# Node phases with the own products made in the edge passes, biases without matmuls and seven table buffers; a convolution whose weighted marks come from GpSimd

## The chip, the cores and the metric

The kernel runs on 1 core of one Trainium2 chip. A core has TensorE (PE: matmuls, its results go to PSUM), VectorE (DVE), ScalarE (ACT), GpSimd (POOL) and SyncE (SP, which here only issues DMAs), and 16 DMA engines that move data between HBM, the chip's large memory, and SBUF, the core's own. Engines run side by side, each through its own list of instructions, and wait for one another on semaphores. The metric is the device time of one execution in microseconds (us), as the median over runs.

## The reference

Four graph layers over N = 6250 nodes with D = 128 features and E = 106250 edges sorted by destination; each is followed by a residual and a layer norm.

```
x = layernorm(x + [x, mean over edges of x[src]] @ W0)                              # layer 0: sum
x = layernorm(x + relu([x, max over edges of msg] @ U1 + c1) @ U2 + c2)             # layer 1: max
      msg = relu([x[src], x[dst], w] @ W1 + b1) @ W2 + b2
x = layernorm(x + sum over edges and loops of (x @ conv_w)[src] * norm + conv_b)    # layer 2: convolution
      norm = dinv[src] * gate * dinv[dst],  gate = sigmoid(gelu([x[src], x[dst]] @ mlp_w1 + mlp_b1) @ mlp_w2 + mlp_b2)
x = layernorm(x + beta mix of (x @ Wskip + bskip) and attention(q, k, v) over edges) # layer 3: attention
```

## The kernel before

Everything is float32 except masks and marks. Nodes are 49 tiles of 128 (NT), taken in 13 batches of four (BT = 4; the last batch has one tile). Edges are 832 tiles of 128, taken in 208 batches of four (BATCHES). The program is a row of phases with a barrier after each: `edges_sum`, `nodes` 0, `edges_max`, `nodes` 1, `edges_gate`, `edges_conv`, `nodes` 2, `edges_attention`, `nodes` 3. Tile names in a profile begin with L, L2a (the gate) or N (a node phase).

**Edge passes.** Four of them gather one row per edge: GpSimd issues one indirect DMA for each of the 832 tiles (`gatherer`, L513) into a ring of eight batches (DEEP), and the other engines turn, scan and store what arrived. `pipeline` writes the software pipeline: at step s an engine does batch s - lag of each of its stages, in the order of the list. A scan (`running_sum`, L616) adds rows of one destination, steered by a mask that is 1 where an edge has the destination of the edge before it.

**The convolution pass** gathers nothing. `edges_gate` has put the rows x @ conv_w of all edges aside in `sent`, so `edges_conv` streams them back (L670, 256 KB a batch), scales each row and scans. The scale of an edge is its gate weight (`ew`) times dinv of its source, looked up by two sets of marks: `hot_low` (L712, which of 128 lanes) goes through TensorE against the table of dinv (`look`, L687, 12 matmuls a batch) and gives 49 candidates for each edge; `hot_high` (L716) marks the right one; VectorE multiplies (L723), sums (L727) and multiplies by the weight (L732). ScalarE scales the rows (L743) and copies the turned sums out (L633). SP issues four DMAs a batch: the lanes `low` and the `mask` (L752, both bf16 and repeated to 128 partitions, 128 KB each), `sent` (L670) and the store of `back` (L624). All of them have rings of four batches (SLOTS).

**Node phases** (`nodes_on`). GpSimd first issues 49 indirect DMAs that fetch the aggregate of each node (`got`, L1386). It then issues 49 that scatter each node's destination table into `seed` (L1477), four to a batch, each batch once its `comb` buffer is filled. Batches go through PE, VectorE and ScalarE with lags of up to six batches: turn the aggregate (L1505), multiply (phase 0: W0x on the node's own x and W0a on the aggregate, L1519 and L1520; phase 1: U1x and U1a, L1511 and L1512, then U2, L1525), layer norm (VectorE L1394 to L1405, ScalarE L1411 and L1418), turn the new x (L1533, copied to `xT` at L1625), make the tables of the next layer (L1545). Biases are added by further matmuls of three bf16 parts against ones (L1526, L1546, L1693). `keep_tables` (L1634, ScalarE) copies the tables from PSUM to `comb`, a ring of three batches (NSLOTS); it waits until the scatter of three batches before has landed. In phase 2 the node's own row x @ conv_w is read back from HBM (`load_xt`, L1488).

## Time and profile before

| | us |
|---|---|
| median of 3 runs | 5461.31 (5458.39 to 5461.77) |
| the profiled execution | 5471.71 |
| its span, first to last instruction | 5470.0 |
| stage: edges_sum, from 0 to 1059.91 | 1059.9 |
| node phase 0, to 1212.52 | 152.6 |
| edges_max, to 2280.03 | 1067.5 |
| node phase 1, to 2469.09 | 189.1 |
| edges_gate, to 3539.55 | 1070.5 |
| edges_conv, to 4096.05 | 556.5 |
| node phase 2, to 4258.26 | 162.2 |
| edges_attention and node phase 3, to the end | 1211.7 |

A stage here begins with GpSimd's first instruction in it. Over the span PE is busy 66%, VectorE 65%, ScalarE 28%, GpSimd 64%. Such averages hide the stages: each has its own limit, and is read on its own. In the rows below a time stands first, then a duration, the engine (a q behind it means its queue, which issues DMAs), the line, the operation, output<-inputs and the shape; what stands in brackets is the idle time before it and what ended it. `issue` means that the engine waited for nothing that the profile shows.

### The profile page before, as it was taken

The page shows a single profiled execution, that of the slowest core. Times are in us where ns is not written, and L with a number is a line of the kernel's source. Part 1 is how long each engine was busy: PE and PEld are TensorE (multiplying, and loading weights), DVE is VectorE, ACT ScalarE, POOL GpSimd, SP SyncE. Part 2 cuts the span into 40 slices and gives each one's busy share as a digit, 9 for nine tenths or more (in the row PEclk, how much of TensorE's full clock was granted, in tenths as well). Part 3 has the DMA queues.
Part 4 walks back from the last instruction along what each step waited for, and adds up shares of the span by engine and source line. Part 5 has one row for each costly group of instructions (what it writes and reads, how often), then busy time and mean ns, then how long its engine had stood idle before and what let it go on. Part 6 is the DMA issues. An engine that isn't in the chain of part 4 may idle for free. (4 is left out here: it accounts for less than half of the span.)

```text
span 5470.0 us, 86641 instructions
## 1 busy us (share of the span) xinstructions
PE 3630.2 (66%) x19277; PEld 2699.7 (49%) x19277; DVE 3535.5 (65%) x7296; ACT 1505.4 (28%) x3630; POOL 3508.5 (64%) x3697
## 2 busy tenths in 40 slices
PE   4444333466666666677888888766656688888883
PEld 3333333344443444345666666555542466666662
DVE  6555222227888878615777777799883466666667
ACT  1111111132222222232222222266664122222222
POOL 7777777667777777647777777500006777777763
PEclk7555555568888888765555555598885677777775
DMA  7555555436666667426666666599983676677761
GB/s 234 182 183 180 188 186 179 140 92 198 206 209 208 207 208 207 138 63 164 172 170 170 171 170 169 140 307 306 290 277 116 190 215 213 214 212 218 215 187 50
DMA packets 832058, 1031.70 MB, mean 189 GB/s; under 512 B 233279, under 2 KB 544079, under 8 KB 831954
## 3 DMA queue, kind: packets, MB, share of 16 engines
q1 hardware_dynamic: 482964, 483.11, 29.0%
q0 software_dynamic: 144320, 323.10, 22.6%
q10 hardware_dynamic: 204670, 224.39, 11.6%
q8 instruction: 30, 0.49, 0.0%
q14 instruction: 74, 0.61, 0.0%
HBM read 668.65 MB, written 361.50 MB: 188 GB/s over the span
## 5 line engine op out<-in xcount | busy, mean ns | idle before, releaser
L513 POOL DMA_INDIRECT L_gath<-tab,src x832 | 796.4, 957 | 256.5 <-issue 250.9
L513 POOL DMA_INDIRECT L_gath<-in_x,src x832 | 789.1, 948 | 255.9 <-issue 251.8
L513 POOL DMA_INDIRECT L_gath<-tab_kv,src x832 | 788.9, 948 | 253.6 <-issue 240.2
L513 POOL DMA_INDIRECT L2a_gath<-tab_h,src x832 | 788.3, 947 | 253.8 <-issue 253.8
L616 DVE TENSOR_TENSOR_SCAN L_acc<-L_mask,L_acc,L_pT 128x512 f32<-128x512 bf16 x414 | 527.5, 1274 | 568.5 <-PE L_pT L574 567.5
L1386 POOL DMA_INDIRECT N_got<-run,last x196 | 190.0, 969 | 664.2 <-POOLq L116 605.6
L633 ACT ACTIVATE L_back<-L_pB 128x512 f32<-128x512 f32 x624 | 364.3, 584 | 894.5 <-PE L_pB L604 888.5
L574 PE MATMUL L_pT<-ident,L_gath 128*128 128x128 f32 x832 | 227.4, 427 | 558.9 <-DMA L_gath<-in_x,src 550.0
L604 PE MATMUL L_pB<-ident,L_acc 128*128 128x128 f32 x2496 | 522.8, 349 | 0.8 <-DVE L_acc L616 0.5
L604 PEld LDWEIGHTS L_pB<-ident,L_acc 128*128 128x128 f32 x2496 | 412.1, 185 | 154.0 <-issue 151.9
L574 PEld LDWEIGHTS L_pT<-ident,L_gath 128*128 128x128 f32 x832 | 146.3, 214 | 637.8 <-DMA L_gath<-in_x,src 340.1
L810 PE MATMUL L_pM<-L_hid,w_W 128*128 128x512 f32 x416 | 295.2, 799 | 175.6 <-DVE L_acc L842 175.0
L928 PEld LDWEIGHTS L2a_pZ<-w_M,L2a_hid 64*128 64x128 f32 x1664 | 370.1, 325 | 79.5 <-issue 79.5
L928 PE MATMUL L2a_pZ<-w_M,L2a_hid 64*128 64x1 f32 x1664 | 387.7, 351 | 0.0
L820 DVE SCALAR_TENSOR_TENSOR L_sent<-b_W1w,L_weight,L_gath 128x128 f32<-128x128 f32 x832 | 235.7, 344 | 204.8 <-DMA L_gath<-tab,src 204.3
L1181 PE MATMUL L_pR<-L_pv,L_same 128*128 128x132 f32 x1664 | 335.8, 364 | 40.0 <-DVE L_pv L1253 37.0
L851 ACT ACTIVATE L_hid<-L_pre 128x512 f32<-128x512 f32 x208 | 131.0, 630 | 834.9 <-DVE L_pre L835 834.9
L955 DVE TENSOR_TENSOR_SCAN L2a_dest<-L2a_same,L2a_dest,L2a_pS 64x512 f32<-64x512 bf16 x207 | 262.8, 1270 | 143.6 <-PE L2a_pS L915 143.6
L1181 PEld LDWEIGHTS L_pR<-L_pv,L_same 128*128 128x128 f32 x1664 | 293.3, 262 | 64.7 <-DVE L_pv L1253 39.4
L921 PE MATMUL L2a_pA<-ident,L2a_gath 128*64 128x128 f32 x832 | 215.1, 414 | 162.9 <-DMA L2a_gath<-tab_h,src 162.9
L1226 DVE TENSOR_TENSOR L_prod<-L_pQ,L_gath 128x512 f32<-128x512 f32 x208 | 143.8, 691 | 269.6 <-DMA L_gath<-tab_kv,src 217.9
L743 ACT ACTIVATE L_scaled<-L_sent,L_scale 128x128 f32<-128x128 f32 x832 | 265.8, 390 | 184.9 <-DVE L_scale L732 181.5
(283 smaller groups left out, 7276.5 us busy)
## 6 DMA issues: line engine op xcount, KB each, us to landing
run<-L_back ACTq DMA_DIRECT2D x416, 256.0 KB, 4.0
L_seed<-seed SPq DMA_DIRECT2D x416, 256.0 KB
run<-L_back ACTq DMA_DIRECT2D x208, 264.0 KB
L_mask<-same SPq DMA_DIRECT2D x416, 128.0 KB, 3.9
seed<-L_zeros SPq DMA_DIRECT2D x208, 256.0 KB, 4.0
sent<-L2a_gath ACTq DMA_DIRECT2D x208, 256.0 KB, 2.9
L_sent<-sent SPq DMA_DIRECT2D x208, 256.0 KB, 4.6
run<-L_back SPq DMA_DIRECT2D x208, 256.0 KB, 4.5
```

The costliest lines, as they stand in the source:

```text
L513: gp.indirect_dma_start(out=gath[k][:, t, :], out_offset=None, in_=table, in_offset=bass.IndirectOffsetOnAxis(ap=g["src"][:, tile:tile + 1 ...
L574: m = pe.transpose(pT[k % 2][:, cols(t)], gath[k][:, t, :], g["ident"][:, :])
L604: m = pe.transpose(pB[k % 2][:, cols(t)], acc[k][:, cols(t)], g["ident"][:, :])
L616: v.tensor_tensor_scan(acc[k][:, :], mask[k][:, :], pT[k % 2][:, :], start_of(acc, n, k), ALU.mult, ALU.add).then_inc(s_scan, 1)
L633: act.activation(rows(back[k][:, :, :]), pB[k % 2][:, :], ACT.Copy).then_inc(s_back, 1)
L743: a = act.activation(scaled[k][:, t, :], sent[k][:, t, :], ACT.Copy, scale=scale[k][:, t:t + 1])
L810: pe.matmul(pM[k % 2][:, :], w["W2"][:, :], hid[k][:, :], start=True, stop=True).then_inc(s_msg, 1)
L820: a = v.scalar_tensor_tensor(sent[k % SLOTS][:, cols(t)], g["wide"]["W1w"][:, :], weight[:, bass.ds(n * BT + t, 1)], gath[k][:, t, :], ALU ...
L921: m = pe.transpose(pA[k % 2][H, cols(t)], gath[k][:, t, H], g["ident"][:, :])
L928: m = pe.matmul(pZ[k % 2][:, t:t + 1], hid[k % SLOTS][:, cols(t)], w["M2"][:, :], start=True, stop=True)
L955: v.tensor_tensor_scan(dest[k][:, :], same[k][:, :], pS[k % 2][H, :], start_of(dest, n, k), ALU.mult, ALU.add).then_inc(s_dest, 1)
L1181: m = pe.matmul(pR[half][:, at:at + W3], same[k][:, cols(t)], pv[k % 2][:, t, :], start=True, stop=True)
```

## The change

- **Own products in the passes.** x @ W0x is made in `edges_sum`, between stretches of its second half, and added to x in SBUF; x @ U1x + c1 is made at the head of `edges_max` (13 matmuls and 13 ScalarE activations ahead of the pipeline) and written over `xT`; node phase 1 adds it with one VectorE operation a batch (`add_own`). conv_b is added to x at the head of `edges_gate` (13 VectorE adds). In node phase 1 ScalarE writes the rows x @ conv_w over `xT` (`own_rows`), from where phase 2 reads them, without `load_xt`.
- **Biases.** b1, c1 and m1 are the bias operand of an activation; c2 is added to x on VectorE (once a batch in phase 1); the bias of the k, v and q tables is added by VectorE as it takes them out of PSUM (`keep_biased`, four operations a batch in phase 2 in place of ScalarE's four copies). Only bskip stays a matmul.
- **Tables in flight.** `comb` has seven buffers (COMBS). The memset of its padding moves from GpSimd to VectorE, and SP's stores have no lag.
- **Convolution.** GpSimd makes `hot_high` with the gate weight already in it, one operation for each tile (`weigh_high`, 832 in all, 128x49 float32 with two per-partition scalars); VectorE's L716 and L732 are gone. The mask is stored once more as bytes (`same8`) and loaded for four batches at once (256 KB), in a ring of two.

```diff
+            for first, end, parts in stretches:
+                for n in parts:
+                    room(pe, s_added, n, 1)
+                    for t in tiles_of(n):
+                        m = pe.matmul(pX[0][:, cols(t - n * BT)], g["xT"][:, cols(t)], g["w"]["W0x"][:, :], start=True, stop=True)
+                    m.then_inc(s_own, 1)
+                pipeline(pe, end, DEEP, [(0, turn), (2, ret)], first=first)
...
+                    v.tensor_tensor(mine, pX[0][:, 0:m * P].rearrange("p (t f) -> p t f", t=m), mine, ALU.add).then_inc(s_added, 1)
...
-            pipeline(sp, BATCHES, SLOTS, [(0, mask_load(sp, g["low"], low, s_low, s_hotl)), (0, load),
-                                          (2, mask_load(sp, g["same"], mask, s_mask, s_scan)), (8, store_rows(sp, run, back, s_back, s_out))])
+            def load_mask(n, k, r):
+                if k % SLOTS == 0:
+                    room(sp, s_scan, n + SLOTS - 1, DEEP)
+                    sp.sem_inc(s_mgo, 1)
+                    sp.dma_start(mask[k // SLOTS][:, :], g["same8"][bass.ds(n * BE, SLOTS * BE)].unsqueeze(0).to_broadcast([P, SLOTS * BE])).then_inc(
+                        s_mask[k // SLOTS], 16)
+            pipeline(sp, BATCHES, DEEP, [(0, on_short(mask_load(sp, g["low"], low, s_low, s_hotl))), (0, on_short(load)),
+                                         (1, load_mask), (8, on_short(store_rows(sp, run, back, s_back, s_out)))])
...
+            def weigh_high(n, k, r):
+                room(gp, s_part, n, SLOTS)
+                for t in range(BT):
+                    tile = n * BT + t
+                    a = gp.tensor_scalar(hot_high[k][:, t, :], row[:, :], high[:, tile:tile + 1], ew[:, tile:tile + 1], ALU.is_equal, ALU.mult)
+                a.then_inc(s_hoth, 1)
+            steps(BATCHES, SLOTS, [(0, weigh_high)])
...
-            pipeline(v, BATCHES, SLOTS, [(0, hot), (1, pick), (0, hot_of_high), (1, gather_up), (3, running_sum(v, pT, mask, acc, s_turn, s_mask, s_ret, s_scan)),
-                                         (1, times_weight)])
+            pipeline(v, BATCHES, DEEP, [(0, on_short(hot)), (1, on_short(pick)), (3, scan), (1, on_short(gather_up))])
...
+            for n in range(NB):
+                room(pe, s_kept, n, 2)
+                m = len(tiles_of(n)) * P
+                pe.matmul(pB[n % 2][:, 0:m], w["U1x"][:, :], g["xT"][:, n * BE:n * BE + m], start=True, stop=True).then_inc(s_own, 1)
...
-    comb = slot("comb", [P, BT, cw])
+    comb = [ph.sb(f"comb{k}", [P, BT, cw]) for k in range(COMBS)]
...
-            pe.matmul(pU[:, 0:count(n) * P], w["U1x"][:, :], g["xT"][:, flat(n)], start=True, stop=False)
-            pe.matmul(pU[:, 0:count(n) * P], w["U1a"][:, :], aT[k][:, 0:count(n) * P], start=False, stop=True).then_inc(s_u, 1)
+            pe.matmul(pU[:, 0:count(n) * P], w["U1a"][:, :], aT[k][:, 0:count(n) * P], start=True, stop=True).then_inc(s_u, 1)
...
-                    pe.matmul(pY[:, cols(t)], g["xT"][:, cols(n * BT + t)], w["W0x"][:, :], start=True, stop=False)
-                    m = pe.matmul(pY[:, cols(t)], aT[k][:, cols(t)], w["W0a"][:, :], start=False, stop=True)
+                    m = pe.matmul(pY[:, cols(t)], aT[k][:, cols(t)], w["W0a"][:, :], start=True, stop=True)
...
+                v.tensor_tensor(comb[k][:, j, 0:fw], pT[j][:, 0:fw], wide["kvq"][:, :], ALU.add).then_inc(s_comb, 1)
```

**PE in node phase 0.** One step in the middle of the phase, before and after (N_pA: aggregate turned; N_pX: new x turned; N_pY: the layer's result; N_pT: tables).

```order
L1505 MATMUL N_pA<-ident,N_agg 128x128 x4
L1533 MATMUL N_pX<-ident,x 128x128 x4
L1519 MATMUL N_pY<-w_W0x,xT 128x128
L1520 MATMUL N_pY<-w_W0a,N_aT 128x128
...
L1545 MATMUL N_pT<-w_W,xT 128x256
L1546 MATMUL N_pT<-bias,ones 128x128
...
```

```order
L1555 MATMUL N_pA<-ident,N_agg 128x128 x4
L1579 MATMUL N_pX<-ident,x 128x128 x4
L1568 MATMUL N_pY<-w_W0a,N_aT 128x128 x4
L1589 MATMUL N_pT<-w_W,xT 128x256 x4
L1555 MATMUL N_pA<-ident,N_agg 128x128 x4
```

Before, each pair stood four times in a step; of 16 matmuls behind the turn of x eight are left.

**VectorE in node phase 2.** One step before and after (N_st, N_mv, N_inv, N_off: the norm's statistics).

```order
L1580 TENSOR_TENSOR N_base<-x,b_conv_b 128x512
L1582 TENSOR_TENSOR N_base<-N_base,N_part 128x512
L1586 SCALAR_TENSOR_TENSOR N_y<-N_got,N_weight,N_base 128x128 x4
L1394 BN_STATS N_st<-N_y 128x6 x4
L1397 BN_AGGR N_mv<-N_st 128x2 x4
L1404 RECIPROCAL N_inv<-N_std 128x4
L1405 SCALAR_TENSOR_TENSOR N_off<-N_mv,N_inv 128x4
```

```order
L1636 TENSOR_TENSOR N_base<-x,N_part 128x512
L1640 SCALAR_TENSOR_TENSOR N_y<-N_got,N_weight,N_base 128x128 x4
L1448 BN_STATS N_st<-N_y 128x6 x4
L1451 BN_AGGR N_mv<-N_st 128x2 x4
L1458 RECIPROCAL N_inv<-N_std 128x4
L1459 SCALAR_TENSOR_TENSOR N_off<-N_mv,N_inv 128x4
L1656 TENSOR_TENSOR N_comb<-N_pT,b_kvq 128x384 x4
```

The add of conv_b has left the step, and the four table copies that stood on ScalarE (L1634) now end it on VectorE.

**VectorE in the convolution.** One batch of the loop before and after.

```order
L712 TENSOR_SCALAR L_hotl<-L_low,L_lane 128x512
L723 TENSOR_TENSOR L_part<-L_pL,L_hoth 128x196
L716 TENSOR_TENSOR L_hoth<-L_row,L_high 128x196
L727 TENSOR_REDUCE L_found<-L_part 128x4
L616 SCALAR_TENSOR_TENSOR L_acc<-L_mask,L_acc,L_pT 128x512
L732 TENSOR_TENSOR L_scale<-L_found,ew_sb 128x4
```

```order
L754 TENSOR_SCALAR L_hotl<-L_low,L_lane 128x512
L760 TENSOR_TENSOR L_part<-L_pL,L_hoth 128x196
L772 SCALAR_TENSOR_TENSOR L_acc<-L_mask,L_acc,L_pT 128x512
L765 TENSOR_REDUCE L_scale<-L_part 128x4
L754 TENSOR_SCALAR L_hotl<-L_low,L_lane 128x512
```

Six operations a batch have become four; the scale of a batch is still ready only behind the scan (in these listings the scan is printed as SCALAR_TENSOR_TENSOR).

## Rows read from the trace of the kernel before

**Rows 1.** Stages: length, busy us of PE, PEld, DVE, ACT, POOL, clock, DMA share, GB/s

```profile
1059.91:1212.52 152.61, 99.38 (x441) 69.42 (x441) 36.33 (x150) 50.35 (x114) 95.25 (x98) 0.72 0.23 64
...
1212.52:2280.03 1067.51, 676.52 (x2912) 440.53 (x2912) 848.26 (x1456) 232.43 (x416) 796.39 (x833) 0.83 0.68 205
...
2280.03:2469.09 189.06, 134.44 (x444) 73.55 (x444) 44.53 (x164) 56.35 (x126) 97.05 (x102) 0.70 0.20 60
...
3539.55:4096.05 556.50, 365.54 (x4160) 300.31 (x4160) 492.39 (x1254) 366.46 (x1040) 0.26 (x2) 0.87 0.92 294
...
4096.05:4258.26 162.21, 95.47 (x196) 34.91 (x196) 51.16 (x201) 65.94 (x173) 96.59 (x99) 0.58 0.41 119
```

**Rows 2.** The page's groups: busy, mean ns of one | idle before, releasers

```profile
L513 POOL DMA_INDIRECT L_gath<-in_x,src x832 | 789.1, 948 | 255.9 <-issue 251.8 <-DMA src<-in_src 2.6 <-PE L_pT L574 1.5
...
L1477 POOL DMA_INDIRECT seed<-N_comb,first x147 | 145.4, 989 | 163.1 <-ACT N_comb L1634 126.2 <-issue 36.9
```

**Rows 3.** Order of time, PE in node phase 0: start, duration

```profile
1122.12 0.65 PE L1533 MATMUL N_pX<-ident,x 128*128 128x128 f32 x4 [2.30 <-ACT x L1418]
...
1125.53 1.06 PE L1545 MATMUL N_pT<-w_W,xT 128*128 128x256 f32 x2
...
1127.32 0.23 PE L1546 MATMUL N_pT<-bias,ones 3*128 3x128 bf16 x1
...
1127.47 0.70 PE L1545 MATMUL N_pT<-w_W,xT 128*128 128x256 f32 x2
...
1129.04 0.66 PE L1505 MATMUL N_pA<-ident,N_agg 128*128 128x128 f32 x4
...
1132.00 0.66 PE L1533 MATMUL N_pX<-ident,x 128*128 128x128 f32 x4 [2.31 <-ACT x L1418]
```

**Rows 4.** Order of time, PE in node phase 1

```profile
2350.85 0.66 PE L1533 MATMUL N_pX<-ident,x 128*128 128x128 f32 x4 [2.87 <-ACT x L1418]
...
2351.34 1.49 PE L1511 MATMUL N_pU<-xT,w_U1x 128*128 128x512 f32 x2
...
2352.63 1.91 PE L1512 MATMUL N_pU<-N_aT,w_U1a 128*128 128x512 f32 x2
...
2363.51 0.90 PE L1533 MATMUL N_pX<-ident,x 128*128 128x128 f32 x3 [2.88 <-ACT x L1418]
```

**Rows 5.** Order of time, GpSimd and ScalarE in node phase 2

```profile
4159.04 1.02 POOL L1477 DMA_INDIRECT seed<-N_comb,first  x1 [0.30 <-issue]
...
4165.24 1.25 ACT L1634 ACTIVATE N_comb<-N_pT 128x384 f32<-128x384 f32 x3 [14.37 <-DMA seed<-N_comb,first]
```

**Rows 6.** Order of time, VectorE and SP's queue in the convolution

```profile
3803.51 1.27 DVE L616 TENSOR_TENSOR_SCAN L_acc<-L_mask,L_acc,L_pT 128x512 f32<-128x512 bf16 x1
...
3803.93 0.33 SPq L752 DMA_DIRECT2D L_mask<-same  x1
...
3804.51 0.36 SPq L624 DMA_DIRECT2D run<-L_back  x1
...
3805.28 0.35 DVE L716 TENSOR_TENSOR L_hoth<-L_row,L_high 128x196 bf16<-128x196 bf16 x1
...
3805.82 1.27 DVE L616 TENSOR_TENSOR_SCAN L_acc<-L_mask,L_acc,L_pT 128x512 f32<-128x512 bf16 x1
```

**Rows 7.** DMA in the convolution, 400 us: queue share; issues, KB, us to landing

```profile
q1 hardware_dynamic: 88065, 120.29, 94.1%
...
L_mask<-same SPq DMA_DIRECT2D x153, 128.0 KB, 4.4
```

**Rows 8.** Order of time, ScalarE in the convolution: four rows scaled

```profile
3804.94 1.28 ACT L743 ACTIVATE L_scaled<-L_sent,L_scale 128x128 f32<-128x128 f32 x4 [1.30 <-DVE L_scale L732]
```

**Rows 9.** Order of time, GpSimd: an iota, and a fetch beside a VectorE add

```profile
3539.64 0.18 POOL L678 IOTA L_row_i<- 128x49 int32 x1
...
4140.48 0.69 DVE L1580 TENSOR_TENSOR N_base<-x,b_conv_b 128x512 f32<-128x512 f32 x1 [1.08 <-ACT x L1418]
...
4140.76 1.23 POOL L1386 DMA_INDIRECT N_got<-run,last  x1 [0.30 <-issue]
```

More of the change, by code:

```diff
@@ L546, in edges_sum @@
         half = beside.STEPS
+        s_own, s_added = ph.sem("own"), ph.sem("added")
+        turns = [half + j * 2 * DEEP for j in range(5)] + [BATCHES]
+        stretches = [(turns[j], turns[j + 1], range(3 * j, min(3 * j + 3, NB))) for j in range(5)]
         block = ph.block()
@@ L588, in _ @@
             beside.vector_after(v)
-            pipeline(v, BATCHES, DEEP, [(0, scan)], first=half)
+            for first, end, parts in stretches:
+                for n in parts:
+                    need(v, s_own, n)
+                    m = len(tiles_of(n))
+                    mine = g["x"][:, n * BT:n * BT + m, :]
+                    v.tensor_tensor(mine, pX[0][:, 0:m * P].rearrange("p (t f) -> p t f", t=m), mine, ALU.add).then_inc(s_added, 1)
+                pipeline(v, end, DEEP, [(0, scan)], first=first)
         @block.scalar
@@ L1463, in scattered @@
     def scattered(n):
[L1464 removed]
+        return 16 * sum(count(q) for q in range(n % COMBS, n + 1, COMBS))
     @block.gpsimd
     def _(gp):
[L1468 to L1470 removed]
         fetch_rows(gp, index, table, got, s_got, s_go)
@@ L1555, in _ @@
         v.memset(eps[:, :], EPS).then_inc(s_eps, 1)
+        if cw > fw:
+            for k in range(COMBS):
+                v.memset(comb[k][:, :, fw:cw], 0.0).then_inc(s_pad, 1)
         if layer == 2:
```

168 lines of the change are left out of this document (98 added, 70 removed).

## The prediction

> **What bounds the kernel now.** I first read the stages [rows 1], then for each stage the wait that ends last. The four passes that gather are not in these rows, because their limit is in one: GpSimd issues 832 indirect DMAs at 0.95 us each with 255.9 / 832 = 0.31 us of plain issue between them, that is 1.25 us each and 1045 us a pass, and almost none of its idle time has another releaser [rows 2]. Such a pass of about 1060 us is GpSimd's list of issues. Work that the change adds there on PE, VectorE or ScalarE is free as long as the ring of eight batches (8 x 5.0 = 40 us of issues) covers it. The change can win in two other places: the convolution, 556.5 us, and the three node phases, 152.6 + 189.1 + 162.2 = 503.9 us.
>
> In a **node phase** GpSimd has 49 fetches and then 49 scatters, the latter at 0.989 + 0.30 = 1.29 us [rows 2, 5]. So the floor of a phase is 49 x 1.25 + 49 x 1.29 = 124.5 us, plus the way out, which no row shows and which I take as 4 us. The rest is waiting: 126.2 us of GpSimd's idle time in front of scatters was ended by ScalarE's copy into `comb` [rows 2].
> - Phase 0: from one turn of x to the next 9.88 us pass (1122.12 to 1132.00) [rows 3], twice the 5.16 us in which GpSimd scatters a batch. PE works from 1122.12 to 1129.04, then waits 2.3 us for ScalarE's norm: PE and ScalarE take turns, so what PE loses shortens the step in full.
> - Phase 1: the same loop, 12.66 us (2350.85 to 2363.51) [rows 4].
> - Phase 2: the first scatter starts at 4159.04, and only at 4165.24 can ScalarE fill the fourth buffer, after 14.37 us of waiting for a scatter to land [rows 5]. Three buffers are full long before the fetches end, and the pipeline that ran ahead stands still.
>
> In the **convolution** four things are nearly level. 153 batches in 400 us are 2.61 us a batch, in which the DMA engines are 94.1% busy, so 2.46 us of DMA time [rows 7]. VectorE, when it does not wait, goes from scan to scan in 2.31 us (3803.51 to 3805.82), and SP needs 0.58 us for each DMA that it issues without a gap (3803.93 to 3804.51), 2.32 us for four [rows 6]. What ties them is a loop through latency: `low` of batch n+5 is issued behind `sent` of n+4, which waits until ScalarE has scaled batch n; the scale of n is ready two VectorE periods after `low` of n is used. Over five batches: 5T = 2T + 1.28 (scaling [rows 8]) + 0.1 + 3 x 0.58 (mask, store, low) + 4.4 (landing [rows 7]), so T = 2.51; it is 2.61, 4% above.
>
> **Node phases, part by part.** Phase 0: between 1122.12 and the first table at 1125.53 lie the turn (0.4) and eight products, 3.0 us; W0x is half of them, 1.5 us. A bias matmul puts the next table 0.15 us later (1127.32 to 1127.47), four are 0.6 us [rows 3]. The step becomes 9.88 - 2.1 = 7.8 us. Seven or eight steps run so, the last four have no result and lose only the biases (up to 0.23, the duration of one, each): 7 x 1.9 (a little less than 2.1, since some of PE's time in a step is spent at its lower clock level whatever stands there) + 3, that is 16 us. A new limit is close: the floor of 124.5 us and the way out leave at most 24 us of 152.6. Phase 1: U1x stands from 2351.34 to 2352.63, 1.3 us [rows 4]; eight bias matmuls at 0.15 are 1.2 us. Against that ScalarE copies the own rows of the second bank ahead of the norm, which I take as one 128x128 activation, 1.28 / 4 = 0.3 us [rows 8]. Net -2.2 us for six steps, 13 us; the start, seven steps without scatters, some 5 us; the tail 2 us: 20 us. The added VectorE operations (c2, `add_own`, about 0.7 each like the add in [rows 9]) lie in PE's time: VectorE is busy 44.5 of 189 us [rows 1]. Phase 2: with seven buffers no batch waits for a scatter until the eighth. PE is busy 95.5 us for 13 batches, 7.3 us each, with biases; VectorE 51.2, 3.9 us each, which becomes 3.9 - 0.69 + 4 x 0.52 = 5.3 us with the table copies (384 columns against 512 in 0.69) [rows 1, 9]. The first table stands four steps of 5.0 us behind the first fetched batch, near 4121; 12 x 7.3 later is 4209, before 4221, where GpSimd itself ends: 4159.04 + 48 x 1.29 = 4221, and the stage, which now ends at 4258.3, ends near 4225: 33 us. This term is the surest, since neither engine's price can move it unless a step exceeds 8 us. The seven buffers also matter in phase 0, where batches 3 to 6 would otherwise wait. Sum of the phases: 69 us.
>
> PE's clock is granted at 0.72, 0.70 and 0.58 of 2.4 GHz on average over the three phases [rows 1], so a mixture of its two levels (1.2 and 2.4). With less work in it PE may be granted the lower one more. Both levels show in a step: the first table's pair of passes takes 1.06 us, a later one 0.70 [rows 3]. At the lower level throughout, the 4.9 us that PE keeps in phase 0 would become 4.9 x 1.06 / 0.70 = 7.4, the step 10.3: nothing gained there but the start and the tail, 3 us, and in phase 1 likewise about 7 us. So the nodes' range is 43 to 75 us.
>
> **The passes.** U1x ahead of `edges_max` is 13 matmuls of 1.3 to 1.9 us [rows 4]: 17 to 25 us by which VectorE's first scan is late, under the 40 us of the ring; VectorE is 79% busy in that pass [rows 1] and catches up. The stretches in `edges_sum` stop the pipeline for three times four matmuls and an add, some 8 us each: covered. If the cover were gone, each would cost its length. The adds of conv_b in the gate are 13 x 0.69 us beside gathers, and a fetch beside such an add took 1.23 us in place of 0.95 [rows 9]: 13 x 0.28 = 3.6 us at most, straight onto a pass bound by issues; I take 2. At the start ScalarE issues as many DMAs as before, but six of them now fill 128 partitions; between 0 and 6 x 0.36 [rows 6], and since a gather already waits for PE's first turn (1.5 us [rows 2]) I take 1. The mask as bytes costs one store and one copy ahead of that, hidden.
>
> **Convolution.** VectorE loses L716 (0.35, 0.27 from start to start) (half of the 0.54 from its start to the scan's) and L732, 0.06: 2.31 - 0.33 = 1.98 us [rows 6]. SP issues 3.25 DMAs a batch: 1.9 us. DMA: 704 KB for 768, and 416 packets for 512; by bytes 2.46 x 0.92 = 2.26 us, by packets 2.00. The loop: 3T = 1.28 + 0.1 + 2.25 x 0.58 + 4.4, T = 2.36; with the same 4% above it 2.46. As the queue is shorter, the landing should fall; at 4.0 us T = 2.23, or 2.32. I take 2.35: 208 x (2.61 - 2.35) = 54 us. Bounds: 2.1 (the DMA time between its two ends), 106 us; 2.55, 12 us.
>
> The price of one mark on GpSimd is in no row. From below: an iota of 128x49, which reads nothing, 0.18 us; from above: an indirect DMA, 0.95 us [rows 9, 2]. I take 0.25, near the iota, since shape and engine are the same and it adds one input and two scalars; four are 1.0 us in 2.35, hidden behind the rest. VectorE's lookup uses them one batch later, so they may lag.
>
> Sum: 5471.7 (profiled execution) - 69 - 54 + 2 + 1 = 5351.7. The median of the runs is 10.4 us under the profiled one: **5341**.
>
> **Rivals.**
> - The convolution stays at the landing of its DMAs. For: 94% busy DMA engines, and now masks that arrive as bursts of 256 KB. Against: fewer bytes and issues. T = 2.55 to 2.61, total 5341 + 48 = 5389. Chance 0.13.
> - It goes further, to the DMA time itself, T = 2.1: 5341 - 52 = 5289. For: VectorE and SP both drop below 2.0. Chance 0.14.
> - PE is granted less clock: the node phases give 43 us in place of 69, total 5367. It lies in my range. Chance 0.12.
> - The marks bind: GpSimd becomes the engine of the convolution, T = 4m for a mark of m us. From m = 0.65 the convolution gains nothing, and as the rest saves 66 us, the whole is slower from T = 2.61 + 66/208 = 2.93, m = 0.73, well inside my two ends. At the upper end, 0.95, T = 3.8 and the total is 5341 + 54 + 208 x 1.19 = 5643. Against: GpSimd's nearest compute row is at 0.18. Chance 0.09, half of it on the slower side.
> - The seven buffers do nothing in phase 2 because a copy of 128x384 on VectorE waits for its other work: a step above 8 us; at 9, 12 us less. Total 5353. Chance 0.05, inside the range.
>
> The Trainium skill (GPSIMD Engine Reference, Engine selection) speaks against this change, for it wants elementwise work on VectorE and calls one-input work on GpSimd roughly line rate and two-input work about 2x slower. And the skill (SBUF — State Buffer, Who interferes with whom) says that a two-port VectorE operation and a GpSimd one lock each other out for a whole instruction; [rows 9] agree in kind, with 0.28 us lost beside an add of 0.69. By that rule each batch would add VectorE's two-port `hot_low` to GpSimd's list, T = 4m + 0.35, and the slower side would begin at m = 0.65 in place of 0.73; at m = 0.25 it changes nothing.
>
> **How the numbers follow.** Forecast 0.47; the rivals as above. The range 5285 to 5395 takes in the forecast, the deeper gain, the convolution that stays and the lower clock, and leaves out the marks (0.09) and what I did not think of, about 0.15 together. Faster than before by over 0.2% (11 us, about what a measurement of this kernel can tell from no change) 0.94; within it 0.02; slower 0.04.
>
> **What would show it.** Phase 2: 129 us, GpSimd without a gap between fetches and scatters, no wait of a table copy for a scatter. Phase 0: steps of 7.8 us, 135 us. Phase 1: steps near 10.4 us, about 169 us. Convolution: about 502 us, VectorE from scan to scan above 1.98, marks near 0.25 apart, DMA about 90% busy. Passes: the same to 3 us. I am wrong if marks stand over 0.6 us apart, if GpSimd's gathers wait for PE at the head of `edges_max`, or if `low` still lands 4.4 us after its issue with VectorE waiting for it in most batches.

## The result, and the profile after

| | before | after |
|---|---|---|
| median of 4 runs, us | 5460.97 (5458.39 to 5461.77) | 5380.89 (5379.49 to 5392.99) |
| span of the profiled execution | 5470.0 | 5391.3 |

The ratio is 0.9854, with a 95% interval from 0.9842 to 0.9865. The kernel became 80 us faster, where the forecast was 120 (5341 us); the time lies in the range of 5285 to 5395, 14 us below its upper end.

By stage, first instruction of GpSimd to the next stage's first:

| stage | before | after | difference | forecast |
|---|---|---|---|---|
| edges_sum | 1059.9 | 1061.9 | +2.0 | +1 |
| node phase 0 | 152.6 | 128.1 | -24.5 | -16 |
| edges_max | 1067.5 | 1068.8 | +1.3 | 0 |
| node phase 1 | 189.1 | 189.0 | -0.1 | -20 |
| edges_gate | 1070.5 | 1072.5 | +2.0 | +2 |
| edges_conv | 556.5 | 527.1 | -29.4 | -54 |
| node phase 2 | 162.2 | 129.8 | -32.4 | -33 |
| attention and phase 3 | 1211.7 | 1214.1 | +2.4 | 0 |

Phase 2 came as forecast and phase 0 gave more; two terms failed: all of phase 1 and nearly half of the convolution. The three node phases together gave 57 us where 69 were forecast. The view by stretches, which answers to [rows 1] with the same columns (node phase 0, edges_max, node phase 1, edges_conv, node phase 2):

```profile
1061.88:1189.98 128.10, 61.43 (x295) 51.96 (x296) 36.52 (x150) 50.34 (x114) 95.38 (x98) 0.75 0.26 76
1189.98:2258.78 1068.80, 689.21 (x2938) 448.16 (x2936) 847.53 (x1459) 259.72 (x429) 797.15 (x833) 0.84 0.69 205
2258.78:2447.77 188.99, 97.28 (x320) 67.85 (x320) 60.97 (x195) 62.42 (x151) 97.12 (x99) 0.66 0.20 60
3520.28:4047.42 527.14, 348.06 (x4160) 302.75 (x4160) 423.03 (x839) 369.75 (x1041) 443.13 (x834) 0.86 0.89 285
4047.42:4177.18 129.76, 53.09 (x147) 29.54 (x147) 64.97 (x235) 45.31 (x124) 97.76 (x99) 0.68 0.41 124
```

Phase 1 is the odd one. PE's busy time fell there by 37 us (134.4 to 97.3), as much as in phase 0 (99.4 to 61.4), yet only phase 0 became shorter. The page's groups, as in [rows 2], say who made GpSimd wait for the tables, and the same view of phase 1 alone says where:

```profile
L1529 POOL DMA_INDIRECT seed<-N_comb,first x147 | 145.1, 987 | 104.7 <-ACT N_comb L1698 60.4 <-issue 43.3 <-DMA seed<-N_comb,first 0.9
...
L1529 POOL DMA_INDIRECT seed<-N_comb,first x49 | 48.3, 985 | 74.8 <-ACT N_comb L1698 59.8 <-issue 14.7 <-DMA seed<-N_comb,first 0.3
```

Of the 126.2 us before, 60.4 are left, and 59.8 of them are in phase 1. In phases 0 and 2 GpSimd now waits 0.6 us in all.

In order of time, PE in phase 0, answering to [rows 3]; the step from N_pX to N_pX is 7.58 us here, and ScalarE's copies of the tables (L1698) of the next two steps start 6.17 and 6.16 us after the last:

```profile
1108.54 1.11 PE L1579 MATMUL N_pX<-ident,x 128*128 128x128 f32 x4 [2.45 <-ACT x L1472]
1109.45 1.91 PE L1568 MATMUL N_pY<-w_W0a,N_aT 128*128 128x128 f32 x8
1111.15 2.08 PE L1589 MATMUL N_pT<-w_W,xT 128*128 128x256 f32 x8
1113.07 0.60 PE L1555 MATMUL N_pA<-ident,N_agg 128*128 128x128 f32 x4
1116.12 0.66 PE L1579 MATMUL N_pX<-ident,x 128*128 128x128 f32 x4 [2.45 <-ACT x L1472]
```

In phase 1, answering to [rows 4], with VectorE among the rows:

```profile
2327.80 1.11 PE L1579 MATMUL N_pX<-ident,x 128*128 128x128 f32 x4 [3.24 <-ACT x L1472]
...
2328.71 1.91 PE L1561 MATMUL N_pU<-N_aT,w_U1a 128*128 128x512 f32 x2
2330.66 0.69 DVE L1622 TENSOR_TENSOR N_u<-N_pU,xT 128x512 f32<-128x512 f32 x1 [3.96 <-PE N_pU L1561]
2331.27 0.68 DVE L1614 TENSOR_TENSOR N_agg<-N_got,b_b 128x512 f32<-128x512 f32 x1
...
2332.59 0.68 DVE L1616 TENSOR_TENSOR x<-x,b_c 128x512 f32<-128x512 f32 x1
2333.20 0.68 DVE L1632 TENSOR_TENSOR N_y<-N_pY,x 128x512 f32<-128x512 f32 x1
...
2333.93 2.08 PE L1572 MATMUL N_pY<-w_U,N_uT 128*128 128x128 f32 x8 [3.31 <-DVE N_y L1632]
...
2335.80 2.44 PE L1589 MATMUL N_pT<-w_M,xT 128*128 128x256 f32 x8
...
2341.91 0.55 PE L1579 MATMUL N_pX<-ident,x 128*128 128x128 f32 x3 [3.24 <-ACT x L1472]
```

The step is 14.11 us, longer than before. Read it from the second wait of PE, 3.31 us at 2333.93. PE would make the next result, but the only PSUM buffer for results, `pY`, is emptied by VectorE's sum (L1632). That stands behind three operations of `prep` (L1614 to L1616), which stand behind `add_own` (L1622), which waited 3.96 us for the product that PE itself made just before. The change took U1x off PE, and tied PE's next product to VectorE's whole list.

Phase 2, answering to [rows 5]: GpSimd goes from the last fetch straight into the scatters, and it waits for no table.

```profile
4110.58 0.95 POOL L1440 DMA_INDIRECT N_got<-run,last  x1 [0.30 <-issue]
4111.84 1.03 POOL L1529 DMA_INDIRECT seed<-N_comb,first  x1 [0.31 <-issue]
```

The copies that fill the tables, here the first, the seventh and the eighth batch, and below them those of the first three batches before the change (the first copy of each):

```profile
4072.18 1.03 DVE L1656 TENSOR_TENSOR N_comb<-N_pT,b_kvq 128x384 f32<-128x384 f32 x2
...
4105.67 1.94 DVE L1656 TENSOR_TENSOR N_comb<-N_pT,b_kvq 128x384 f32<-128x384 f32 x4
...
4118.04 1.95 DVE L1656 TENSOR_TENSOR N_comb<-N_pT,b_kvq 128x384 f32<-128x384 f32 x4 [6.93 <-DMA seed<-N_comb,first]
```

```profile
4120.11 0.49 ACT L1634 ACTIVATE N_comb<-N_pT 128x384 f32<-128x384 f32 x1 [1.75 <-PE N_pT L1546]
...
4131.74 0.49 ACT L1634 ACTIVATE N_comb<-N_pT 128x384 f32<-128x384 f32 x1 [1.75 <-PE N_pT L1546]
...
4143.36 0.49 ACT L1634 ACTIVATE N_comb<-N_pT 128x384 f32<-128x384 f32 x1 [1.75 <-PE N_pT L1546]
```

All seven buffers are full before the first scatter, and the eighth batch and four later ones wait for a scatter to land, 15.5 us in all. The steps also differ: batches follow one another 5.4 us apart where they were 11.6 us apart before, and that is so before any copy had waited for a scatter.

The convolution, 400 us from 3600, answering to [rows 6, 7]: the DMA view, the waits of SP's queue (total, times, longest), and the groups of the marks and of `hot_low`:

```profile
q1 hardware_dynamic: 75547, 116.43, 90.5%
...
L_low<-low SPq DMA_DIRECT2D x161, 128.0 KB, 4.4
```

```profile
SPq L696 <- ACT L_scaled L783: 94.6, 83, 2.9
```

```profile
L718 POOL TENSOR_SCALAR L_hoth<-L_row,L_high,ew_sb 128x49 f32<-128x49 bf16 x649 | 345.6, 561 | 55.5 <-DVE L_part L760 55.4
...
L754 DVE TENSOR_SCALAR L_hotl<-L_low,L_lane 128x512 bf16<-128x512 bf16 x162 | 57.1, 353 | 67.6 <-DMA L_low<-low 67.2
```

162 batches in 400 us are 2.47 us each. A mark costs 0.56 us on average, not 0.25, so GpSimd is 86% busy. But VectorE waits 67 us for `low`, which still lands 4.4 us after its issue, and SP waits for ScalarE's scaling before it may issue `sent`, more than twice as long as before (94.6 us for 40.2, in the same view of before). So there were two suspects: the marks, and the loop through the loads.

### The profile page after: what moved, and what is told of

It is laid out like the page before. It is cut to its first block and busy times, and to the rows that moved or that the text cites. A ratio compares the mean times of both kernels' runs of the same rounds, so it can differ in the third digit from the quotient of the medians.

```text
span 5391.3 us, 85535 instructions
## 1 busy us (share of the span) xinstructions
PE 3515.6 (65%) x19081; PEld 2691.1 (50%) x19081; DVE 3509.0 (65%) x6976; ACT 1541.4 (29%) x3619; POOL 3954.8 (73%) x4526
## 5 line engine op out<-in xcount | busy, mean ns | idle before, releaser
L641 DVE TENSOR_TENSOR_SCAN L_acc<-L_mask,L_acc,L_pT 128x512 f32<-128x512 bf16 x207 | 264.8, 1279 | 537.0 <-PE L_pT L587 536.2
L718 POOL TENSOR_SCALAR L_hoth<-L_row,L_high,ew_sb 128x49 f32<-128x49 bf16 x832 | 442.9, 560 | 67.1 <-DVE L_part L760 65.2
L897 ACT ACTIVATE L_hid<-L_pre,b 128x512 f32<-128x512 f32 x208 | 150.1, 722 | 795.5 <-DVE L_pre L881 795.5
L1062 ACT ACTIVATE L2a_hid<-L2a_pre,m 64x512 f32<-64x512 f32 x208 | 150.1, 722 | 640.8 <-DVE L2a_pre L1015 597.7
L1200 PE MATMUL L_pQ<-L_seed,L_same 128*128 128x128 f32 x1664 | 317.5, 349 | 0.0
```

The source lines that it names most:

```text
L641: v.tensor_tensor_scan(acc[k][:, :], mask[k][:, :], pT[k % 2][:, :], start_of(acc, n, k), ALU.mult, ALU.add).then_inc(s_scan, 1)
L718: a = gp.tensor_scalar(hot_high[k][:, t, :], row[:, :], high[:, tile:tile + 1], ew[:, tile:tile + 1], ALU.is_equal, ALU.mult)
L1200: m = pe.matmul(pQ[k % 2][:, cols(t)], same[k][:, cols(t)], seed[h][:, cols(t)], start=True, stop=True)
```

## The experiments

Each kernel is the changed kernel with one edit, unless said otherwise. Stages are read as above. Their spread where the code is the same matters for the small ones: the convolution stood between 527.1 and 537.5 us in six profiles of the same code (mean 531.9), phase 1 between 184.4 and 189.0 in five. The first eight ran on chips on which the kernel before takes 5472 to 5476 us. The last four ran on two slower chips, on which it takes 6771 us (the first three) and 6769 us (loads_eight_tables_three): there the edge passes that gather are 19 to 37% longer and the node phases longer too, and the reason was not looked for. These four are compared only with each other and with before on their chip. The convolution is the same there (532.0 us). n1_no_own_copy, n1_prep_last, marks_half, marks_narrow, low_bytes and tables_three were executed once each, the others four or five times; each stage is read from one execution.

| kernel | phase 0 | phase 1 | conv | phase 2 | median | before there |
|---|---|---|---|---|---|---|
| n1_sums_earlier | 127.9 | **140.8** | 537.5 | 128.8 | 5348.06 | 5475.55 |
| n1_u1x_on_pe | 127.6 | **154.8** | 530.3 | 129.0 | 5352.34 | 5475.55 |
| n1_no_own_copy | 128.1 | 183.8 | 530.1 | 129.2 | 5383.05 | 5475.55 |
| n1_prep_last | 127.8 | 185.8 | 534.0 | 128.7 | 5396.19 | 5475.55 |
| marks_half | 127.6 | 185.6 | 534.7 | 128.7 | 5388.06 | 5471.83 |
| marks_narrow | 128.1 | 186.4 | 532.3 | 129.9 | 5388.74 | 5471.83 |
| marks_vector | 127.9 | 184.9 | **541.0** | 128.5 | 5399.05 | 5471.83 |
| masks_old | 127.6 | 184.4 | **546.2** | 129.2 | 5398.01 | 5471.83 |
| loads_eight | 158.3 | 178.8 | **460.5** | 147.0 | 6570.55 | 6770.80 |
| low_bytes | 160.6 | 219.8 | 529.6 | 143.5 | 6672.86 | 6770.80 |
| tables_three | 159.3 | 218.4 | 532.0 | 142.6 | 6675.83 | 6770.80 |
| loads_eight_tables_three | 161.8 | 175.8 | **455.1** | 145.2 | 6587.02 | 6768.59 |

### Phase 1: what stands in the chain

**n1_sums_earlier**

```diff
-1: [(0, prep), (3, gather_up), (4, turned), (0, add_own)]       # VectorE
+1: [(0, prep), (2, gather_up), (3, turned), (0, add_own)]
-1: [(0, turn_agg), (5, turn_new), (0, hidden), (1, result), (6, tables)]    # PE
+1: [(0, turn_agg), (4, turn_new), (0, hidden), (1, result), (5, tables)]
...                                                  # ScalarE's lags likewise
```

> Node phase 1 of the changed kernel with the sums (gather_up, turned and the steps behind them on ScalarE and PE) one step of the list earlier, as in phase 0. Theory: phase 1 stayed at 189.0 us because add_own stands last in VectorE's step and waits for PE's hidden product, and the sum that gives back the only PSUM buffer of the results stands behind it, with three operations of prep between; PE's result then waits for all of them. With the sum ahead of add_own the chain is cut: steps fall from 13.0-14.2 to 10-11 us, the phase to 167-175 us, the whole by 14 to 22 us. Rival: ScalarE's additional own-row copies, or PE's lower clock, make the step: the phase stays within 186-191 us.

Phase 1 fell to 140.8 us, by 48 us and far below the 167 to 175 expected. The ratio to before is 0.977 (0.9754 to 0.9786). In order of time, a step of PE and VectorE:

```profile
2340.28 0.66 PE L1579 MATMUL N_pX<-ident,x 128*128 128x128 f32 x4 [3.24 <-ACT x L1472]
...
2340.77 1.24 PE L1561 MATMUL N_pU<-N_aT,w_U1a 128*128 128x512 f32 x2
...
2341.80 1.92 PE L1572 MATMUL N_pY<-w_U,N_uT 128*128 128x128 f32 x8
...
2342.04 0.69 DVE L1622 TENSOR_TENSOR N_u<-N_pU,xT 128x512 f32<-128x512 f32 x1 [2.86 <-PE N_pU L1561]
...
2344.57 0.68 DVE L1632 TENSOR_TENSOR N_y<-N_pY,x 128x512 f32<-128x512 f32 x1
```

PE's result (L1572) now starts as soon as the hidden product ends, ahead of `add_own`. The wait of 3.31 us is gone; ScalarE's copies of the tables of successive steps start 9.56, 7.90, 8.72 us apart. The work is the same, so the cause of the failed term is the order of the lists. Why it gave more than expected was not tested; I had compared with the step of before, not with one that has neither U1x nor biases nor the wait.

**n1_u1x_on_pe**

```diff
+            pe.matmul(pU[...], w["U1x"][:, :], g["xT"][:, flat(n)], start=True, stop=False)
-            pe.matmul(pU[...], w["U1a"][:, :], aT[k][...], start=True, stop=True).then_inc(s_u, 1)
+            pe.matmul(pU[...], w["U1a"][:, :], aT[k][...], start=False, stop=True).then_inc(s_u, 1)
...
-            act.activation(uT[k][...], u[k][...], ACT.Relu)
+            act.activation(uT[k][...], pU[...], ACT.Relu, bias=g["c1"][:, 0:1])
```

> One part undone: in phase 1 PE makes x's product with U1x again in the same group as the aggregate's, ScalarE adds c1 in its relu, VectorE has no add_own, and the product is not made ahead of the max pass. Everything else is as changed. Theory (add_own is the new wait): the step is that of before without eight bias products, 12.66 - 1.2 + 0.4 for the own-row copies, near 11.9 us; phase 1 falls from 189.0 to 176-182 us although PE has 1.3 us more to do in a step. Rival (ScalarE's copies or the clock): with more on PE the phase becomes 189 to 198 us. The max pass: the same within 2 us, if the prelude was covered.

154.8 us, again below the 176 to 182 expected: with more work on PE the phase is 34 us shorter, and 34 us shorter than before the change too. Even against the other profiles of equal code (184.4 at least) it is 30 us. This kernel keeps the lags, so it shows the same cause without moving any stage: as it was put, the addition cost far more than the product that it saved. The row of PE also prices the biases. Below, eight results' and eight tables' passes in this kernel, and then the same place before the change, with biases (2354.33 to 2359.98):

```profile
2321.86 1.89 PE L1581 MATMUL N_pT<-w_M,xT 128*128 128x256 f32 x8
2323.59 0.60 PE L1546 MATMUL N_pA<-ident,N_agg 128*128 128x128 f32 x4
...
2331.17 1.35 PE L1564 MATMUL N_pY<-w_U,N_uT 128*128 128x128 f32 x8
2332.36 0.81 PE L1581 MATMUL N_pT<-w_M,xT 128*128 128x256 f32 x3
```

```profile
2354.33 0.64 PE L1525 MATMUL N_pY<-w_U,N_uT 128*128 128x128 f32 x2
...
2356.94 0.70 PE L1545 MATMUL N_pT<-w_M,xT 128*128 128x256 f32 x2
...
2359.98 0.66 PE L1505 MATMUL N_pA<-ident,N_agg 128*128 128x128 f32 x4
```

Before, the two take 5.65 us; here 1.19 + 1.73 = 2.92. That is 2.73 us for eight biases, 0.34 each where I took 0.15. Some of it is the clock, whose granted mean in the phase is 0.80 of 2.4 GHz here and 0.70 before, both a mixture of its two levels (1.2 and 2.4). The max pass is 1065.3 us without U1x's products at its head, and 1065.6 to 1071.1 with them in eight profiles: they are covered, or cost up to 3 us on average.

**n1_no_own_copy**: leaves out L1701, whose copies phase 2 reads.

> Leaves out ScalarE's copies of the own rows in phase 1 (two of 0.38 us in a step), so phase 2 adds other rows there; its time is that of the same work otherwise. Theory (add_own chain): ScalarE is not in the chain of most steps, phase 1 stays within 185-189 us. Rival (ScalarE is what lengthens the step): 0.8 us in each of 13 steps, phase 1 at 178-181 us.

183.8 us, against 184.4 to 189.0 with the copies: no difference that these profiles can tell, and above the 178 to 181 of the rival. Those copies did not make the step; the two runs above say the same.

**n1_prep_last**

```diff
-1: [(0, prep), (3, gather_up), (4, turned), (0, add_own)]
+1: [(3, gather_up), (4, turned), (0, prep), (0, add_own)]
```

> Only the order of VectorE's list in phase 1: sum, turned, prep, add_own, in place of prep, sum, turned, add_own. It takes prep's three operations (1.9 us) from between add_own and the sum. Theory: the step loses up to 1.9 us, but prep now stands behind the statistics (1.5-2 us) and holds the next aggregate's turn, so part comes back: phase 1 175-188 us. Rival (add_own and prep are not in the chain): 189 us or more, up to 200 as prep comes later.

185.8 us: inside the spread too, so no gain of this order can be seen. That the later aggregate took back prep's 1.9 us is a guess. The value lies in the theory's range and 3 us below the rival's, less than the spread of equal code, so it tells little apart.

### The convolution: the marks, the masks, the loads

**marks_half**

```diff
-                for t in range(BT):
+                for t in range(BT // 2):
```

> GpSimd makes the marks of two tiles of each batch in place of four; the other two tiles' marks are zeros written once, so half of the scales are left out of the sum, and every other step is unchanged. Theory A (the mis-sized mark sets the convolution: 4 x 0.54 = 2.16 us of 2.53): the stage falls from 527-537 us to 490-505 us, T near 2.35, as forecast with small marks. Theory B (the DMAs' landing or VectorE set it, and the marks have 16% of slack): 520-537 us, no change.

534.7 us, no change. The groups of the same 400 us: GpSimd now idles 233 us of them, and VectorE still waits 77 us for `low`.

```profile
L720 POOL TENSOR_SCALAR L_hoth<-L_row,L_high,ew_sb 128x49 f32<-128x49 bf16 x318 | 167.2, 538 | 233.4 <-DVE L_part L762 233.4
...
L756 DVE TENSOR_SCALAR L_hotl<-L_low,L_lane 128x512 bf16<-128x512 bf16 x158 | 55.0, 348 | 77.0 <-DMA L_low<-low 76.6
```

Theory A falls: I had mis-sized a mark by a factor of two, and it cost nothing here.

**marks_narrow**

```diff
-  gp.tensor_scalar(hot_high[k][:, t, :], row[:, :], ...)
+  gp.tensor_scalar(hot_high[k][:, t, 0:HIGH // 2], row[:, 0:HIGH // 2], ...)
```

> Each mark on GpSimd is 24 columns wide in place of 49, the other columns are zeros written once (so half of the sources are left out of the scales). If a mark is a fixed price for its instruction, it still lasts 0.45-0.54 us and the stage stays at 527-537 us; if it goes by columns, a mark lasts near 0.3 us and the stage does what it does with half of the marks (theory A: 490-505, theory B: 520-537).

```profile
L720 POOL TENSOR_SCALAR L_hoth<-L_row,L_high,ew_sb 128x24 f32<-128x24 bf16 x639 | 285.4, 467 | 113.9 <-DVE L_part L762 102.2
```

Half of the columns take 0.467 us for 0.56: a mark is mostly a fixed price (about 0.09 us for 25 columns). The stage, 532.3 us, again doesn't move.

**marks_vector** (VectorE's L716 and L732 of before are back, the masks stay bytes) and **masks_old** (masks as bf16, one DMA a batch; the marks stay on GpSimd): each half of the change alone.

> One part undone: VectorE makes the marks (one comparison for the batch) and multiplies with the weights, as before the change; GpSimd does nothing in the convolution; the masks stay bytes for four batches. Theory A (marks on GpSimd bind): VectorE is then at about 2.3 us a batch again without GpSimd beside it, the masks' gain stays: T 2.35-2.5, 490-520 us, faster than the changed kernel's 527-537. Theory B (the marks' move is what brought the gain since VectorE was in the loop): T goes back to 2.55-2.65, 540-556 us.

> The other part undone: masks as bf16, one DMA for each batch, as before the change; the marks stay on GpSimd. Theory A (marks bind, the masks are what helped before): T is then set by SP's four DMAs and 94% busy DMA engines, 2.55-2.65, 540-556 us. Theory B (VectorE's shorter list is the gain): 520-537 us, as with byte masks.

541.0 and 546.2 us. Before the change it was 556.5, with both parts 531.9 on average. So the masks alone bring some 15 us, the marks alone some 10, both 25. With a spread of 10 us in equal code these are rough, and so are the medians: 0.9854 for both, 0.9867 and 0.9865 for one. If one part alone had been the bound, the other would have been worth nothing. With the old masks the DMA engines are 94.3% busy again, as before. The intervals of the two ratios, 0.9849 to 0.9882 (masks_old) and 0.985 to 0.9883 (marks_vector), both overlap with that of the changed kernel (0.9842 to 0.9865), so only the stages tell them apart. Each theory was right in one of the two runs, and something else holds T at 2.5 us.

**loads_eight** (on top of n1_sums_earlier)

```diff
-        mask, low = [...], slot("low", [P, BE], BF16)
+        mask, low = [...], [ph.sb(f"low{k}", [P, BE], BF16) for k in range(DEEP)]
...
+        sent = [ph.sb(f"sent{k}", [P, BT, D]) for k in range(DEEP)]
...
-                room(sp, s_scale, n, SLOTS)
+                room(sp, s_scale, n, DEEP)
...
-                                         (1, load_mask), (8, on_short(store_rows(...)))])
+                                         (5, load_mask), (12, on_short(store_rows(...)))])
```

> Node phase 1 as in n1_sums_earlier, and in the convolution low and sent have eight buffers each in place of four (the mask is loaded, and rows are stored, four steps later in SP's list so that SP doesn't wait for them). What the marks cost plays no part by now, so the question is what holds T at 2.5 us. Theory C (a loop through latency: SP may issue low and sent only when four batches back has been used, and low takes 4.4 us to land): the loop has four more batches to close in, T falls to the next limit, the DMA time of 2.25 us or the marks' 2.2, stage 470-495 us. Theory D (the DMA engines are as full as they get at 90%, longer buffers only lengthen the queue): low lands later, 6 us or more, and the stage stays at 525-540 us.

460.5 us, 71 less than the 532.0 of the same stage on the same chip (tables_three, whose convolution is the changed one). The stage as a whole; then the DMA view, SP's waits and GpSimd's marks in 400 us from 4360:

```profile
4318.73:4779.26 460.53, 313.64 (x4160) 283.05 (x4160) 418.75 (x839) 366.48 (x1041) 443.26 (x835) 0.93 0.96 326
```

```profile
q1 hardware_dynamic: 87299, 134.57, 98.6%
```

```profile
SPq L702 <- ACT L_scaled L789: 24.1, 51, 1.5
```

```profile
L724 POOL TENSOR_SCALAR L_hoth<-L_row,L_high,ew_sb 128x49 f32<-128x49 bf16 x753 | 400.7, 563 | 0.0
```

Theory C holds, and the stage fell further than its 470 to 495. The same bytes and the same marks take 2.14 us a batch, and two limits are reached together: GpSimd makes 753 marks in 400 us without a pause (0.53 us each, 2.13 for four), and the DMA engines are 98.6% busy. SP's wait for the scaling falls from 97.5 us (tables_three, 400 us) to 24.1. Only now does the price of a mark bind. The edit also moves the loads of the mask and the stores four steps later in SP's list; that was not run by itself, but in the changed kernel SP waits for nothing except the scaling (94.6 us of 400), so the order alone had no other wait to remove. Which of `low` and `sent` needs the buffers was not taken apart either. The ratio to before is 0.9702 (0.9685 to 0.9718), with the gain in phase 1 in it: 6570.55 us where the two that differ little from the changed kernel took 6672.86 and 6675.83.

**low_bytes**

```diff
-        ..., slot("low", [P, BE], BF16)
+        ..., [ph.sb(f"low{k}", [P, SLOTS * BE], U8) for k in range(DEEP // SLOTS)]
```

> Everything as changed, but low is loaded as bytes for four batches in one DMA, as the mask is: 64 KB of 704 less for each batch to write, 0.75 of SP's issues less. It is also loaded earlier. Theory C (latency loop): low is out of the loop and sent alone is in it; T 2.25-2.4, 475-505 us. Theory D (bandwidth): T falls by the bytes, 9%: 2.3, 480-495 us; if VectorE's comparison is slower on bytes (0.55 us in place of 0.35) it still waits for nothing else. Neither: the stage stays at 525-540 us.

`low` is stored as bytes and loaded for four batches in one DMA. 529.6 us: no change, where theory C expected 475 to 505 and theory D 480 to 495. In 400 us from 4400:

```profile
q1 hardware_dynamic: 57336, 104.39, 83.4%
```

```profile
L760 DVE TENSOR_SCALAR L_hotl<-L_low,L_lane 128x512 bf16<-128x512 uint8 x160 | 78.0, 488 | 59.3 <-DMA L_low<-low 59.3
```

The DMA engines are at 83% and the stage takes the same time. That speaks against theory D as clearly as loads_eight does. It also corrects theory C: fewer bytes and issues do not take `low` out of the loop, since its DMA stands behind `sent` in SP's list, and `sent` waits for the scaling of four batches back. The trace has this order: `sent` issued at 4608.89 right after a scaling ended, a store at 4609.47, `low` at 4610.08, and at 4615.03 VectorE starts on it after 1.27 us of waiting. SP waits 162.1 us for the scaling in these 400 us, against 97.5 in tables_three. Of the kernels run, only the two with more buffers for `sent` and `low` opened the loop.

### The tables

**tables_three**: `COMBS = 3`.

> One part undone: three comb buffers in place of seven, in all node phases; all else as changed. Theory: phase 2 owes its 32 us to them and returns to 155-165 us; phase 0 owes part of its 24.5 us to them (batches 3 to 6 wait for scatters while GpSimd still fetches): 135-145 us; phase 1, held by add_own, stays at 186-191 us. Rival: the shorter products alone made phase 0, it stays at 128 us.

On the slower chip nothing moves: phase 0 159.3 us against 160.6 with seven (low_bytes), phase 1 218.4 against 219.8, phase 2 142.6 against 143.5. In phase 2 the table copies wait 1.0 us for scatters. Below that group stand the first copies of the second batch of tables and GpSimd's first scatter:

```profile
L1656 DVE TENSOR_TENSOR N_comb<-N_pT,b_kvq 128x384 f32<-128x384 f32 x49 | 24.8, 552 | 14.8 <-PE N_pT L1589 10.7 <-DMA L_low<-low 3.1 <-DMA seed<-N_comb,first 1.0
```

```profile
4937.10 1.02 DVE L1656 TENSOR_TENSOR N_comb<-N_pT,b_kvq 128x384 f32<-128x384 f32 x2
...
4938.54 1.03 POOL L1529 DMA_INDIRECT seed<-N_comb,first  x1 [0.30 <-issue]
```

So the question was not put here. The first batch of tables was filled from 4910.50, the second only from 4937.10, 27 us later, for a reason that the rows don't name; one batch was full when the scatters began, where on the faster chip all seven were. In phase 0 likewise the first table was copied at 1343.30, when the fetches had ended and GpSimd had waited 15.13 us. Three buffers could not run short in such a pipeline at the start. What the run does show is that later, with three buffers, batches follow 5.4 us apart (4956.94, 4962.34, 4967.82).

**loads_eight_tables_three** was meant to ask this again on a faster chip, and fell on another slow one.

> loads_eight (sums of phase 1 a step earlier, eight buffers for low and sent) with three comb buffers in place of seven. The run of loads_eight, and that of tables_three, fell on a chip whose gathers are slower throughout, so this one asks both questions again. Convolution: theory C (latency loop) 465-480 us in place of 527-541 on the faster chips; theory D (bandwidth) 525-540. Phase 2: if the seven buffers brought its 32 us, it returns from 129 to 155-165 us; if VectorE, which now fills the tables and has little else to do there, copes with three (on the slower chip it waited 1.0 us for scatters, the phase stood at 142.6 us against 143.5 with seven), it stays at 129-134 us. Phase 0: 128 us if the shorter products made it, 135-145 us if the buffers did. Phase 1: 141.5 us with seven; 142-152 us with three. Whole, if C holds and the buffers do nothing: 0.966 of before or less; if the buffers matter in all phases: 0.975.

Convolution 455.1 us, for 460.5 with seven (the stage has none of these buffers, and this is within the spread of equal code), so theory C's gain came again on a second chip; phase 0 161.8 for 158.3, phase 1 175.8 for 178.8, phase 2 145.2 for 147.0. The whole is 0.9722 of before (0.9702 to 0.9743), which overlaps with 0.9702 (0.9685 to 0.9718). Here too one batch of tables was full when the scatters of phase 2 began. No effect of the buffers can be told on these chips. On the faster ones, where the phases are shorter by 14 to 38 us, three buffers were not measured.

## Why the prediction was right, and where it failed

The time lies in the range, 40 us above the forecast, and in part by luck. The upper end was set for a convolution that stays and for a lower clock. What filled it was half of the convolution's term (25 us) and a phase 1 that gave nothing (20 us), which no rival had; phase 0 gave back 8.5 us, and the passes took 5 more. Two figures of the prediction have no working: the 75 us at the upper end of the nodes' range, and the chances, which already add up to 1.00 before anything is left for what was not thought of.

- **Node phase 0, forecast -16, measured -24.5.** Mechanism right, size too small. I put a bias at 0.15 us, the distance to the next row; all told it is up to 0.34. With 0.27 (the 2.15 us between steps of 12.66 before and 10.51 in n1_u1x_on_pe, over eight, an estimate), the step is 9.88 - 1.5 - 1.1 = 7.3, and 7.58, 6.17 and 6.16 were seen. The biases explain about half a microsecond of each step beyond the forecast; the rest was not taken apart. GpSimd reached the floor: 128.1 us against 124.5 and a way out of 2.4 (4174.75 to 4177.18 in phase 2).
- **Node phase 1, forecast -20, measured -0.1.** The step that failed is "The added VectorE operations (c2, `add_own`, ...) lie in PE's time: VectorE is busy 44.5 of 189 us". It read a busy share where it should have read an order. I asked what PE gives away, not what stands behind an operation that waits for PE, on an engine whose next operations free PE's only result buffer. n1_sums_earlier shows it: the same work, 44 to 48 us less. Without the wait the phase gives 34 (U1x on PE) to 48 us against before, so the 20 us of the sum were hidden by the wait, and too small besides.
- **Node phase 2, forecast -33, measured -32.4.** The end near 4225 was right in kind because GpSimd's list ends the stage, whatever fills the tables in time. The way there was not as written, and that the number fits is partly luck. "PE is busy 95.5 us for 13 batches, 7.3 us each" took a busy share for a step: before the change the first three batches of tables start 11.6 us apart, with buffers free, and from the wait at 4165.24 to the last copy at 4250.39 the nine steps take 9.5 us on average. Twelve steps from 4120 end at 4259 with 11.6 us and at 4234 with 9.5, so by this estimate more buffers alone could not have ended the stage at 4225. What did is a step of 5.4 us: PE has no biases there, VectorE makes the copies that stood in ScalarE's list, and the granted clock rose from 0.58 to 0.68. Which of these it is was not taken apart. The seven buffers were used (all full before the first scatter), but whether they were needed is open: with three, the fourth batch would have waited until about 4118, and nine steps of 5.4 us more end near 4167, still before GpSimd's last scatters. This too is an estimate, and no run asked it on a fast chip. The sign "no wait of a table copy for a scatter" failed, since the eighth waited 6.93 us; it cost nothing.
- **Convolution, forecast -54, measured -29.4** (-24.7 against the mean of six profiles). The term is T: 2.35 taken, 2.47 measured in mid-stage. The loop through latency was the right model; loads_eight supports it: with more buffers and the same bytes T fell to 2.14. I wrote 2.36 for a landing of 4.4 us, 2.46 with the same 4% above it, and then took less because "as the queue is shorter, the landing should fall". It didn't: `low` lands in 4.4 us at 90.5% as masks did at 94.1% [rows 7], with VectorE waiting for it, which the prediction had named as a sign of being wrong. Without that sentence the forecast is 2.46, -31 us. The rival that the convolution stays at the landing, 2.55 to 2.61, was about as near as the forecast. The price of a mark, 0.25 for 0.56 us, was the largest error in a single number and changed nothing, because it stayed under T; the rival's rule T = 4m appears in loads_eight (4 x 0.53 = 2.13), once the loads are deeper, together with DMA engines that are 98.6% busy.
- **Passes, forecast +3, measured +7.7.** edges_sum +2.0 and gate +2.0 are near. Attention and phase 3 stood between 1208.0 and 1214.2 us in nine profiles of the same code, before at 1211.7: its +2.4 is spread, not an effect. Gathers did wait for PE in edges_sum, 7.0 us in all for 1.5 before.
- **Clock.** The granted mean went from 0.72 to 0.75 in phase 0, from 0.70 to 0.66 in phase 1, and to 0.77 when phase 1 stopped waiting. In phase 2 it rose from 0.58 to 0.68. In phases 0 and 2 PE had less to do and was granted more, so the rival that less work costs clock is not seen there. In phase 1 it fell with less work and longer waits, and n1_u1x_on_pe, with more work, has 0.80 where n1_sums_earlier has 0.77; what sets it is open.

The rule of the Trainium skill that elementwise work belongs on VectorE (GPSIMD Engine Reference, Engine selection) is borne out by the price of a mark, 0.56 us for one tile on GpSimd where VectorE marked four tiles in 0.35 [rows 6], and not by the result: the move was worth some 10 us as long as another chain was longer. Of the lock between a two-port VectorE operation and GpSimd (the Trainium skill, SBUF — State Buffer, Who interferes with whom) the traces show little here: `hot_low` takes 0.353 us beside the marks and 0.349 in marks_vector without them. The add in [rows 9], which the prediction puts beside this rule, reads two tensors and is no two-port operation by that section, so it bears on the rule only loosely.

## What to carry to other kernels

An engine's busy share doesn't say that there is room on it: before putting an operation on an idle engine, ask which operation stands behind it in program order, and whether that one frees a buffer for the engine it waits for. When DMA engines look 90% busy, try the number of buffers before the number of bytes: here 64 KB less a batch did nothing, and four more buffers gave 71 us. Read the length of a step from one row to its next, not from busy time over the number of steps: in phase 2 that was 7.3 us against 11.6. A landing time measured under load should be kept in the sum unless an experiment shows it falling.

## What the runs showed of the hardware

- A 128x49 comparison and multiplication with two per-partition scalars on GpSimd takes 0.56 us (0.53 from start to start when nothing else holds it); with 24 columns it still takes 0.467; an iota of the same shape took 0.18 [rows 9].
- A bias matmul of three rows between pairs of float32 products cost 0.27 to 0.34 us on PE, estimated from the steps with and without it at somewhat different granted clocks; its own record is 0.20 to 0.28 us.
- VectorE's 128x512 comparison takes 0.488 us when it reads bytes and 0.353 when it reads bf16; the scan took 1.27 us with either mask.
- An activation with a per-partition bias takes 0.722 us in edges_max (128x512) and in the gate (64x512); without it, before, 0.630.
- The DMA engines moved 291 GB/s in the changed convolution at 90.5% busy and 337 GB/s in loads_eight at 98.6%.
